# Rest tiles of the probabilities transposed directly behind the main tiles of units two and four, with other PSUM banks and the router's logits behind them

## What is computed

```python
# x: (32, 256, 256), ctx: (32, 77, 512); 16 heads of 64
x = x + tanh(g_xattn[0]) * attention(layernorm(x), ctx, ...)   # q = x Wq / 8; k, v = split(ctx Wkv), with a null key and value
#   sim = q k^T ; attn = softmax(sim) ; out = attn v ; out = layernorm(out Wout) * ln_scale + ln_bias
x = x + tanh(g_ffn[0]) * ffn(layernorm(x), ...)
#   logits = x Wr + br ; aff = sigmoid(logits) ; the 8 largest, divided by their sum, are the weights of 8 experts
#   out = shared expert(x) + sum over the 8 experts of weight * expert(x)
```

## Time and profile before

| | us |
|---|---|
| median of 3 runs | 2158.05 |
| lowest of them | 2155.35 |
| span of the profiled execution, first to last instruction | 2156.4 |
| attention stage, about | 300 to 1180 of the span |
| PE busy in the span | 2034.8 (94%) |
| DVE busy | 1768.4 (82%) |
| ACT busy | 1387.1 (64%) |
| POOL busy | 1204.5 (56%) |

### The profile page before, as it was taken

How to read it: one execution, slowest core, us unless ns; L and a number is a source line. 1 busy time by engine, 2 the same in 40 slices (tenths; PEclk the granted TensorE clock), 3 DMA queues, 4 the chain that set the end, 5 groups by cost and what they waited for, 6 DMA issues and landing times. The chain is left out here.

```text
span 2156.4 us, 43812 instructions
## 1 busy us (share of the span) xinstructions
PE 2034.8 (94%) x14306; PEld 1884.7 (87%) x14306; DVE 1768.4 (82%) x4190; ACT 1387.1 (64%) x4030; POOL 1204.5 (56%) x1324
## 2 busy tenths in 40 slices
PE   7999689999999999999997889999999999999995
PEld 7888589999999999999997778988988888888884
DVE  4544258899999999999997766668999999999996
ACT  3322357677777777777774347777777777777771
POOL 0000202777777777777777600006777777777775
PEclk9999889999999999999998899999999999999997
DMA  9876489988888888788886999999999999999997
GB/s 275 280 242 216 140 240 297 304 262 249 246 252 252 252 249 250 248 249 246 248 259 224 298 360 286 287 285 365 403 403 402 397 397 395 391 392 399 393 366 280
DMA packets 442777, 645.86 MB, mean 300 GB/s; under 512 B 204984, under 2 KB 317337, under 8 KB 440089
## 3 DMA queue, kind: packets, MB, share of 16 engines
q1 hardware_dynamic: 393400, 508.79, 71.0%
q0 software_dynamic: 49152, 134.28, 17.2%
HBM read 325.18 MB, written 317.72 MB: 298 GB/s over the span
## 5 line engine op out<-in xcount | busy, mean ns | idle before, releaser
L1710 POOL DMA_INDIRECT parts<-results_dram,kept_index x512 | 516.1, 1008 | 382.7 <-DMA results_dram<-y 219.0
L848 POOL DMA_INDIRECT pages_dram<-rows,kept_index x512 | 509.4, 995 | 167.0 <-issue 139.1
L927 ACT ACTIVATE exps<-sim,minus_max 128x78 f32<-128x78 f32 x1024 | 320.8, 365 | 50.5 <-DVE minus_max L1028 49.9
L927 ACT ACTIVATION_READ_ACCUMULATOR exps<-sim,minus_max 128x1 f32 x1024 | 252.3, 247 | 0.0
L1731 ACT ACTIVATE w_h<-w_raw 128x768 fp32r<-128x768 f32 x159 | 134.0, 843 | 149.7 <-DMA w_raw<-in_experts 149.7
L1819 DVE SCALAR_TENSOR_TENSOR parts<-parts,kept_weight 128x256 f32<-128x256 f32 x448 | 213.6, 477 | 1.8 <-DMA parts<-dense_dram 0.7
L1916 PE MATMUL xps<-ident,xin 128*128 128x128 f32 x1272 | 167.0, 275 | 18.1 <-DVE wq_l L1781 7.9
L1793 DVE TENSOR_TENSOR w_l<-w_raw,w_h 128x768 fp32r<-128x768 f32 x159 | 151.7, 954 | 38.6 <-ACT w_h L1731 38.4
L140 PE MATMUL yps<-w_h,hid_h 128*128 128x256 f32 x636 | 180.0, 283 | 0.7 <-DVE hid_l L1876 0.7
L142 PE MATMUL yps<-w_l,hid_h 128*128 128x256 f32 x636 | 178.7, 281 | 0.0
L141 PE MATMUL yps<-w_h,hid_l 128*128 128x256 f32 x636 | 178.2, 280 | 0.0
(11 more groups left out here) (270 smaller groups left out, 7206.5 us busy)
## 6 DMA issues: line engine op xcount, KB each, us to landing
xin<-pages_dram SPq DMA_DIRECT2D x159, 512.0 KB, 10.5
results_dram<-y SPq DMA_DIRECT2D x159, 512.0 KB, 9.6
w_raw<-in_experts SPq DMA_DIRECT2D x159, 385.0 KB, 9.5
pages_dram<-blank SPq DMA_DIRECT2D x108, 512.0 KB, 4.0
pages_dram<-blank SPq DMA_DIRECT2D x12, 1536.0 KB, 8.2
values_dram<-values SPq DMA_DIRECT2D x16, 1024.0 KB
v_main<-values_dram SPq DMA_DIRECT2D x64, 256.0 KB
keys_h_dram<-keys_h SPq DMA_DIRECT2D x16, 616.0 KB, 4.8
```

The lines of the kernel that those rows point to most:

```text
L848: pool.indirect_dma_start(dram["pages"], bass.IndirectOffsetOnAxis(ap=kept_index[:, at:at + 1].bitcast(U32), axis=0), buffer(batch)[:, k / ...
L927: last = act.activation(exps[u % 2][:, h, :], scores(u)[:, h // 4, h % 4, :], ACT.Exp, bias=minus_max[u][:, h:h + 1], accum_out=row_sum[u] ...
L1710: pool.indirect_dma_start(parts[slot(batch, t)][:, k, :], None, done, bass.IndirectOffsetOnAxis(ap=kept_index[:, at:at + 1].bitcast(U32), ...
```

## The change

`T1b` moves in `RING` from behind `Q0` to directly behind `T1a`, and `L` follows behind it. `T3a` moves from ahead of `Q2` to behind it, directly ahead of `T3b`. The banks: `T1b` 1 to 2, `L` 2 to 0, `Q0` 0 to 1, `PV0a` 1 to 0, `PV0b` 0 to 1. Since `EVICTED` is made from `RING`, ScalarE and VectorE change their order too. The three parts of the choice of experts that read the logits (`logits`, `top`, `mask`) hang behind `Q0` instead of `T1a`.

```diff
-RING = ["X", "N2", "Oa", "T0a", "Ob", "T1a", "L", "Q0", "T1b", "Q1", "PV0a", "PV0b", "T2a", "R", "T3a", "Q2", "T3b", "Q3",
+RING = ["X", "N2", "Oa", "T0a", "Ob", "T1a", "T1b", "L", "Q0", "Q1", "PV0a", "PV0b", "T2a", "R", "Q2", "T3a", "T3b", "Q3",
         "PV1a", "PV1b"]
-BANK = {"X": 1, "N2": 2, "Oa": 3, "T0a": 0, "Ob": 3, "T1a": 1, "L": 2, "Q0": 0, "T1b": 1, "Q1": 2, "PV0a": 1, "PV0b": 0, "R": 3,
-        "T2a": 2, "T3a": 1, "Q2": 0, "T3b": 3, "Q3": 2, "PV1a": 1, "PV1b": 0}
+BANK = {"X": 1, "N2": 2, "Oa": 3, "T0a": 0, "Ob": 3, "T1a": 1, "T1b": 2, "L": 0, "Q0": 1, "Q1": 2, "PV0a": 0, "PV0b": 1, "T2a": 2,
+        "R": 3, "Q2": 0, "T3a": 1, "T3b": 3, "Q3": 2, "PV1a": 1, "PV1b": 0}
...
-ROUTE_AFTER = {"T1a": ["logits", "top", "mask"], "PV0b": ["placed"], "Q3": ["opened", "page", "moved", "slot"],
+ROUTE_AFTER = {"Q0": ["logits", "top", "mask"], "PV0b": ["placed"], "Q3": ["opened", "page", "moved", "slot"],
...
-                if (name == "T1a" and b >= B) or (name in ("T3a", "PV1b") and b == B):
+                if (name == "Q0" and b >= B) or (name in ("T3a", "PV1b") and b == B):
```

## The result

| | before | changed |
|---|---|---|
| median | 2159.82 us | 2188.06 us |
| lowest | 2155.35 us | 2185.79 us |
| span of the profiled execution | 2156.4 us | 2192.9 us |

The ratio is 1.0146, 95% interval 1.0124 to 1.0169: slower by 28 us, with 2188 us forecast and 2188.06 measured. One of the four executions of before took 8088.35 us: the median in the table counts it, the ratio goes by the other three, whose median is 2158.05, and against that the change costs 30 us. The profiled execution of the changed kernel is the longest of its four (2195.03 us), so its span is 36.5 us longer than that of before and not 28 to 30; where the difference lies is taken up under the prediction's sum.

A forecast was written before the change was run, and what follows sets the result against it. The prediction took a closed PE-VectorE chain through `PV0a`'s wait for `T1b`'s low part as the bound. 29 x 1.02 = 29.6 us on 2156.4 gave 2186.0, plus 1.65 for the median: 2188 us, range 2162 to 2203.

The forecast's parts named there:

- the prediction's sum: 29 iterations at 1.02 us, 29.6 us, odd iterations 0; profiled 2186.0, plus 1.65 for the median: 2187.7, say 2188 us.
- Lost waits: At `PV0a` the 0.34 us wait for `T1b` goes, at `Q2` 0.24; grouping transposes saves 0 to 0.14.
- the prediction's first rival: Not slower: only the gains at `PV0a` remain, 0.34 + 0.05 us per iteration, -11 us, 2147; 8%.
- the last step: From `Q2` to `PV1a`: `PV1a` 1.02 us later, the wait vanished at `Q2` giving back a tenth.
- the prediction's first paragraph: Closed chain per iteration, 27.49 us: `PV0a` to next scores, VectorE's `maximum` to `T1b`'s low part, back to `PV0a`.
- First place: `Q0` now needs `T1a`'s bank: starts at 706.80 instead of 705.89, PE standing still some 0.9 us.
- Second place: `PV0a` now needs `L`'s bank, free after the logits behind `Q0`'s low part: 1.10 us later, PE still some 0.5.
- Second half of the iteration: `Q1`'s low part, `centre` and `PV0a`'s low part 1.11 us later; `PV1a` 1.02 later, so 27.49 becomes 28.51.
- The third rival: Clock: PE's idle 1.4 us per iteration lowers the granted clock; 20 slowed matmuls in each would make 2250; 6%.
- The second rival: Half absorbed, as between scores and `T1a`: 0.2 to 0.5 us per iteration remain, 2164 to 2172; 10%.

The follow-up runs named there:

- pv_banks: Kernel before with only the banks of `PV0a` and `PV0b` exchanged, and those of `T3a` and `Q2`; 2159.64 us, ratio 1.002.
- second_half: Kernel before with only `Q2` moved ahead of `T3a` and the change's banks for `PV0a` and `PV0b`; 2160.98 us, ratio 1.0017.
- q0_bank: Kernel before, step order untouched, with `Q0` given the bank of `T1a`, `T1b` the old bank of `Q0`, others renumbered; 2185.81 us, ratio 1.0136.
- logits_early: Changed kernel with `logits`, `top` and `mask` put back behind `T1a` on VectorE; 2183.08 us, ratio 1.0129.
- centre_first: Kernel before with `Q2` ahead of `T3a`, the change's `PV0a`/`PV0b` banks, `centre` ahead of `normalise(3)`, now behind `PV0a`'s low part; 2150.80 us, ratio 0.9969.

## Why the prediction was right, and where its terms were off

**Lost waits.** The waits named did go: PE has none at `PV0a` for `T1b` and none at `Q2`. But the price that the prediction's first rival put on them, 0.34 and 0.05 us in each iteration, was wrong, and so was the tenth that the last step gave back for `Q2`: pv_banks and second_half show that without them PE waits at `R` for `centre`, and nothing is gained (27.49 and 27.57, against 27.45). So the chain as the prediction's first paragraph has it, closed by `PV0a` waiting for `T1b`'s low part, is not what bounds the kernel before: the chain goes on over VectorE to `centre` and from there to `R`. The rival's 2147 had no ground even if its conditions had held. Grouping saved no restart: `T1a` to `L` is 0.61 us instead of 0.36, 0.25 for a pair that took 0.14 where it stood.

**First place.** Right: `Q0` 2.32 us behind `T1a` where the prediction has 2.30. The stand-still is 0.65 in the row and not 0.9. Of the difference 0.11 went into the grouped transposes. The rest, 0.17, is how the row counts: from the end of the last matmul, which lies 0.28 us behind its start, while the next would have started 0.115 behind it. q0_bank shows that this one bank is enough for the loss.

**Second place.** Right in its times. `Q0` to `PV0a` is 3.47 us (3.46 in the prediction), `T1a` to `PV0a` grew by 1.13 (1.10), PE's wait is 0.40 (0.4 to 0.6), and VectorE's idle time behind `T1a` 0.82 ("up to 1"). In the step from `Q0`'s low part to the logits the row gives 523.19 - 522.58 = 0.61 us, by which the chain was worked out. The Trainium skill (VectorE: DVE Perf Modes, The DRAIN you can't avoid) has the next operation wait until the pipe is empty, and start earlier where it isn't held. The row agrees with the second, 0.61 against a duration of 0.69. The wait itself is worth nothing: logits_early removed it and the loss stayed, as the prediction says in its next part ("even without the second stand-still of PE nothing would be won"). What sets the lateness are `Q0`'s and `Q1`'s low parts, and through them `centre`.

**Second half of the iteration.** The chain by VectorE was right: `Q1`'s low part 1.14 us later (1.11), `R` 9.28 us behind `T1a` (9.20). What was mis-sized lies mostly behind `R`. The prediction has 28.51 - 9.20 = 19.31 us up to the next `T1a`, a tenth less than before; measured are 19.46, a tenth more than the 19.35 of before. Two places make up this 0.15, both at `PV1a`, for which the prediction had named the wait but no further cost:

- `PV1a` waits for `T3a`'s low part, which ends at 530.73 + 0.68 = 531.41, and starts at 531.56: a restart of 0.15 us and not 0.05.
- From `PV1a` to the scores it takes 534.51 - 531.56 = 2.95 us. In the kernel before, where `PV1a` follows `Q3` without a stop at 716.98, it is 2.87:

```profile
719.85 0.24 PE L140 MATMUL sim<-kT_h,qT_h 128*128 128x156 f32 x1
```

`T3a` to `T3b` takes 0.44 as well, where the prediction set 0.36, but PE is ahead of VectorE there and this costs nothing. The 0.15 and the 0.08 at `R` make 0.23, and the rhythm came out as 28.74 instead of 28.51.

**Sum.** The rhythm grew by 1.27 to 1.29 (means and medians) and not by 1.02, and yet the median lies where it was forecast. The first and the last `T1a` with logits behind it, before and then changed, show what the profiled pair did:

```profile
338.18 0.60 PE L1343 MATMUL ring<-ident,probs 128*128 128x128 f32 x4
1144.34 0.60 PE L1343 MATMUL ring<-ident,probs 128*128 128x128 f32 x4
```

```profile
338.99 0.49 PE L1343 MATMUL ring<-ident,probs 128*128 128x128 f32 x3
1179.27 0.60 PE L1343 MATMUL ring<-ident,probs 128*128 128x128 f32 x4
```

The 29 iterations between them took 806.2 us before and 840.3 after, 34.1 more; 0.8 lie ahead of them and 1.6 behind, which makes the 36.5. The first two of the 29 were not in the rhythm (28.3 and 35.8 us before, 28.5 and 35.2 after) and together gave back 0.5; the other 27 cost 1.28 each. So the terms of the sum were 27 x 1.28 and not 29 x 1.02, with 1.9 for everything else where the prediction has 0, and the profiled execution came out 7 us above the 2186.0 that was added up. That the median met the forecast to the microsecond is therefore in part luck: it lies 7 us under the profiled execution, and in the second measurement of the same kernel it was 2193.25. Why executions of the changed kernel differ by some us (2186 to 2196) stays open; both traces are of long ones. Both medians are inside the range, and the mechanism doesn't hang on it. The prediction calls 2%, 43 us, about what a measurement of this kernel can tell from no change; the intervals in the table are 0.2 to 0.5% wide, so far smaller differences can be told.

**Clock.** The third rival falls: with two stand-stills of 0.65 and 0.40 us in each iteration the granted clock stayed at 1.00. The Trainium skill (TensorE: Matmul & The Clock Gate, What's actually happening) has the lower clock as the default that activity lifts; these gaps were not enough to lose it here. The second rival fell as well: nothing was absorbed between the scores and `T1a` (12.15 us before, 12.14 after, medians). The expert stage is unchanged, as said: from the last logits on VectorE to the end it is 944.4 us before and 944.8 after.

## What to carry to other kernels

In a closed loop between two engines, look for the stretch in which one of them has no gap at all (here VectorE from `T1a`'s low part to `centre`): a gap put there costs its whole length and a little more, while the waits that the other engine shows elsewhere may be worth nothing when they are removed. Where a tile leaves a buffer by two engines one after the other, the step that next takes that buffer needs the time of both; with four banks, giving one step the bank of the step two ahead of it cost 1.4%. When two changes each cause the same delay, undoing one shows next to nothing: try each alone from the side of the fast kernel too.

## What the runs showed of the hardware that was not expected

Four transposes followed directly by two more take longer to the next step: 0.44 us from the first to `T1b` or `T3b`, against 0.36 from `T1a` to `L` before. The pair takes 0.17 (518.36 to 518.53) ahead of `L` and 0.14 (529.73 to 529.87) ahead of a query, as before, so this is not a matter of the grouping. A matmul starts 0.05 to 0.06 us behind the end of the operation that it waits for at `Q0`, `PV0a` and `R`, but 0.15 behind it at `PV1a`, in the changed kernel as in centre_first. Why there, no run shows. After such a stop the step takes 0.08 us longer in all (2.95 against 2.87 for `PV1a` and `PV1b`).
